# A fused gated-recurrence and ternary feed-forward block on one core: one weight on another DMA queue, powers ahead of constants, transposes in halves, another order around the second sequence

## The chip, the cores and the metric

The kernel runs on one core of one Trainium2 chip, in one launch. The metric is the device time in microseconds (us) of an execution. The kernel before takes 77.18 us, the median of 3 runs (77.08 to 77.36).

## What is computed

The input x holds 2 sequences of 512 tokens with 256 features, in float32. It is normalised once over its features, and two branches read the result:

```python
xn = (x - mean) / sqrt(var + eps)
# branch 1: gated linear recurrence
y    = gelu(xn @ w_y + b_y)
xb   = xn @ w_x + b_x
conv = conv_b + sum_k conv_w[k] * xb shifted by (3 - k) tokens     # 4 taps
gate_x, gate_a = sigmoid(conv @ w_ig + b_ig), sigmoid(conv @ w_ag + b_ag)
a    = exp(-8 * gate_a * softplus(a_param));  mult = sqrt(1 - a**2)
h_t  = a_t * h_{t-1} + gate_x * conv * mult                        # scan over tokens
attn = (h * y) @ w_out + b_out
# branch 2: feed-forward with ternary weights, hidden size 682
g    = silu(xn @ q(w1).T) * (xn @ q(w3).T)
out  = x + attn + g @ q(w2).T
```

## The kernel before

All is on chip after one load. Five engines each have a hand-written list of instructions, and semaphores tie them: an engine executes its list in order, and a wait in it holds all that stands behind. The source gives one function per engine: `sync` (SP, which issues nearly all DMAs), `gpsimd` (POOL), `scalar` (ACT), `vector` (DVE) and `tensor` (PE).

Exact products are made from a high part and a low part: a value v is rounded to a high part (on ACT), and the low part is v minus it. So there are `xt_hi`, `xt_lo` (the transposed, normalised x), `w_hi`, `w_lo` (five 256x256 weights, numbered WX, WY, WIG, WAG, WOUT) and `conv_hi`, `conv_lo`. A dense product is w_hi with the high part, w_lo with the high part and w_hi with the low part, accumulated in PSUM.

The start, per sequence s (4 tiles of 128 tokens):

1. DVE takes `statistics` (L437) and `variance` (L442, L445) of tiles; POOL raises v_eps to the power -0.5 (`rstd_of`, L231); DVE writes xn (`normalise`, L450). For s = 0 this goes in two halves of two tiles, each with its own power; for s = 1 in one piece, after one DMA for the whole sequence (L188).
2. PE transposes xn against the identity (`transposes`, L642, two per tile); ACT makes xt_hi of each half of the sequence (`xt_hi_of`, L288), DVE xt_lo of it (`xt_lo_of`, L456).
3. PE makes xb: for s = 0 in `first_x_terms` (L749, 256 columns at a time, 24 matmuls), for s = 1 in `dense_terms` (L653). ACT evicts xb with the newest tap and a bias (`newest_tap`, L317), DVE adds the other three taps (`older_taps(s, c)`, L489 and L493, one chunk c of 128 features at a time), ACT rounds it (`conv_hi_of`, L342) and POOL subtracts (`lo_of_conv`, L251).

POOL also makes small constants of the conv (`conv_constants`, L238 to L247: eight operations of 128x2, of which `newest_tap` needs `conv_c` and `older_taps` needs `head`) and `half_b` (L259), and the low parts of the weights (`square_lo`, L226). ACT rounds the weights (`square_hi`, L283) as they land. PE does 12 warm-up matmuls on ones and two more between waits (L722) before its first transpose.

The lists around the change, in the order of execution:

- SP: 4 tiles of x[0], WX, all of x[1], WY, WIG, WAG, w1, w3, w2, WOUT.
- POOL: `conv_constants`, `half_b`, two powers, (wait for xn of s = 0) `square_lo(WX)`, the power of s = 1, `square_lo(WY)`, `square_lo(WIG)`, `square_lo(WAG)`, four `lo_of_conv`.
- ACT: `square_hi(WX)`, `xt_hi_of(0)`, `square_hi(WY)`, `newest_tap(0)`, `square_hi(WIG)`, `xt_hi_of(1)`, the sum of absolute values of w1 (L300), `square_hi(WAG)`, `conv_hi_of(0, 0)`, the same sum of w3, `newest_tap(1)`, `conv_hi_of(0, 1)`, and on with gelu, tanh, exp.
- DVE: statistics and normalise of s = 0, statistics of s = 1, `xt_lo_of(0)`, `normalise(1)`, two tiny operations, `older_taps(0, 0)`, `xt_lo_of(1)`, `older_taps(0, 1)`, `older_taps(1, 0)`, `older_taps(1, 1)`, the thresholds and ternary weights (L460 to L505).
- PE: warm-up, transposes of s = 0, w_hi and w_lo with xt_hi, then w_hi with xt_lo for xb of s = 0; for y of s = 0 w_hi and w_lo with xt_hi, the transposes of s = 1, w_hi with xt_lo; then xb and y of s = 1, and the gates. The second gate of s = 0 reuses the PSUM of xb of s = 1 and so waits for the last `older_taps`.

After the gates come the hidden products of the feed-forward branch (L670), g (DVE, L515), its high and low parts (ACT L338, POOL L256), a tail of 42 hidden units (`tail_lo`, L573), and the products with w2 (`down`, L703) and w_out (L714).

Of the kernel before, what the change touches and what calls it, by code (L numbers as in the profile page):

```python
# [19 lines left out]
P = 128  # L20
# [5 lines left out]
KC = D // P  # L26
# [7 lines left out]
WARM = 12  # L34
# [9 lines left out]
def build(nc: bass.Bass, x, dense, w13t, w2t, params, b_out, out):  # L44
# [7 lines left out]
    with ctx:  # L52
# [85 lines left out]
        x_loaded = [sem(f"x_loaded{i}") for i in range(TILES + 1)]  # L138
# [42 lines left out]
        def _(sp):  # L181
# [5 lines left out]
            square(WX)  # L187
            sp.dma_start(x_sb[:, 1], x_dram[1]).then_inc(x_loaded[TILES], 16)  # L188
# [24 lines left out]
        def _(pool):  # L213
# [19 lines left out]
            def conv_constants():  # L233
# [24 lines left out]
            conv_constants()  # L258
            nc.gpsimd.tensor_scalar(half_b[:, :], par[:, B_IG:B_IG + 2 * KC], 0.5, None, ALU.mult).then_inc(half_b_set, 1)  # L259
            rstd_of(0, slice(0, TILES // 2), 1)  # L260
            rstd_of(0, slice(TILES // 2, TILES), 2)
            pool.wait_ge(xn_set, TILES)
            square_lo(WX)
            rstd_of(1, slice(0, TILES), 3)
            square_lo(WY)
            square_lo(WIG)
# [162 lines left out]
        def _(dve):  # L429
# [155 lines left out]
            dve.wait_ge(x_loaded[TILES], 16)  # L585
            statistics(1, range(TILES))
            variance(1, range(TILES))
            xt_lo_of(0)
            normalise(1, range(TILES), 3)
# [46 lines left out]
        def _(pe):  # L636
            def transposes(s):

                for t in range(TILES):
# [7 lines left out]
            def dense_terms(dst, m, terms, first, last, chunk_ready=None):  # L647
                for c in range(KC):
# [71 lines left out]
            def warm(count):  # L720
                for _ in range(count):
                    nc.tensor.matmul(slot[WARM_SLOT][:, 0, 0:P], ones[:, :], ones[:, :], start=True, stop=True)  # L722
# [20 lines left out]
            def first_x_terms(weights, part, ready):  # L743
                for h in range(2):
                    pe.wait_ge(ready, h + 1)
                    for c in range(KC):
                        for o in range(KC):
                            for w in weights:
                                mm = nc.tensor.matmul(slot[X_SLOT[0]][:, o, halves[h]], w[:, WX, c, o * P:(o + 1) * P],  # L749
                                                      part[:, 0, c, halves[h]],  # L750
                                                      start=(part is xt_hi and h == 0 and c == 0 and w is w_hi),
                                                      stop=(part is xt_lo and c == KC - 1), skip_group_check=True)
# [91 lines left out]
```

## Time and profile before

| | us |
|---|---|
| median of 3 runs | 77.18 (77.08 to 77.36) |
| the profiled execution, its own time | 77.82 |
| span of its trace, first to last instruction | 76.0 |
| busy: PE, DVE, ACT, POOL | 70.0, 60.8, 49.9, 33.4 |

The profile is of one execution. It has a page of summaries, and the trace behind it answers finer questions: the busy time of each engine in a stretch, the chain of instructions that ended last, and the instructions in order of time with their waits. Matmuls are pipelined: a matmul's stated duration holds its modelled end, so the pace is read from the distance between starts. The granted clock is 1.00 throughout.

### The profile page before, as it was taken

To read this page: it belongs to the slowest core of one execution; us is meant where nothing else is said; L and a number is where in the kernel's file an instruction comes from. 1 tells how busy PE (TensorE), PEld (TensorE's weight loads), DVE (VectorE), ACT (ScalarE), POOL (GpSimd) and SP (SyncE) were. 2 spreads that over 40 slices of the span, in tenths; PEclk is the share of its full clock that TensorE was granted. 3 is DMA by queue.
4 is the path that set the end of the run, shared out by engine and by line. 5 is a ranking of instruction groups with operands and counts; after the bars stand their busy time and mean duration, and the time that the engine had idled before them with its cause. 6 is when DMAs were issued, how large, how long until landed. Compare 5 with 4: busy or idle time off the path is not lost.

```text
span 76.0 us, 1062 instructions
## 1 busy us (share of the span) xinstructions
PE 70.0 (92%) x364; PEld 60.1 (79%) x364; DVE 60.8 (80%) x99; ACT 49.9 (66%) x76; POOL 33.4 (44%) x43
## 2 busy tenths in 40 slices
PE   4999879999999799999999999499999999999960
PEld 4999768877887678888888889388888888899950
DVE  4887599999999999999989999169999999400340
ACT  3663714899999999999989768996357429100000
POOL 6385646336661750052007968940007818910000
DMA  0989999910000000000000000000000000340062
GB/s 13 259 212 338 349 405 367 361 67 9 0 0 0 4 0 0 0 0 0 5 1 0 0 9 0 0 0 0 0 0 0 0 0 0 111 165 9 0 207 69
DMA packets 5095, 5.63 MB, mean 74 GB/s; under 512 B 525, under 2 KB 4578, under 8 KB 5090
## 3 DMA queue, kind: packets, MB, share of 16 engines
q1 hardware_dynamic: 4946, 5.55, 21.8%
q8 instruction: 3, 0.05, 0.2%
q10 hardware_dynamic: 144, 0.01, 0.1%
q14 instruction: 2, 0.02, 0.1%
HBM read 4.51 MB, written 1.05 MB: 73 GB/s over the span
## 4 chain that ended last, share of the span: by engine, by line
PE 37%; ACT 33%; DVE 9%; DMA 7%; issue 5%; POOL 3%; SPq 3%; DVEq 0%; ACTq 0%
PE slot L670 12%; PE slot L703 11%; PE slot L714 9%; DMA x_sb<-x 7%; ACT ta L363 4%; POOL g_lo L256 3%; ACT tx L349 3%; ACT conv_hi L342 3%; ACT xn_y L324 3%; PE slot L653 2%; ACT ta L355 2%; SPq L186 2%; ACT g_hi L300 2%; DVE w_raw L515 2%; DVE stats L437 2%
## 5 line engine op out<-in xcount | busy, mean ns | idle before, releaser
L256 POOL TENSOR_TENSOR g_lo<-w_raw,g_hi 128x512 fp32r<-128x512 f32 x10 | 15.9, 1609 | 16.1 <-ACT g_hi L338 16.1
L670 PE MATMUL slot<-xt_lo,w_q 128*128 128x512 f32 x40 | 15.7, 394 | 0.0
L670 PE MATMUL slot<-xt_hi,w_q 128*128 128x512 f32 x40 | 15.7, 393 | 0.0
L703 PE MATMUL slot<-w_q,g_hi 128*128 128x256 f32 x40 | 10.2, 292 | 1.1 <-POOL g_lo L256 1.1
L703 PE MATMUL slot<-w_q,g_lo 128*128 128x256 f32 x40 | 9.8, 282 | 0.0
L332 ACT ACTIVATE w_raw<-slot,scale 128x512 f32<-128x512 f32 x10 | 6.8, 686 | 4.3 <-PE slot L670 4.3
L493 DVE SCALAR_TENSOR_TENSOR conv<-slot,par,conv 128x511 f32<-128x511 f32 (+2 forms) x12 | 9.0, 748 | 0.4
L703 PEld LDWEIGHTS slot<-w_q,g_hi 128*128 128x128 f32 x40 | 7.6, 191 | 1.6 <-POOL g_lo L256 1.6
L670 PEld LDWEIGHTS slot<-xt_lo,w_q 128*128 128x128 f32 x40 | 7.5, 188 | 1.7
L670 PEld LDWEIGHTS slot<-xt_hi,w_q 128*128 128x128 f32 x40 | 7.5, 188 | 1.7
L338 ACT ACTIVATE g_hi<-w_raw 128x512 fp32r<-128x512 f32 x10 | 6.3, 630 | 3.4 <-DVE w_raw L515 3.2
L552 DVE TENSOR_TENSOR x_sb<-slot,x_sb 128x512 f32<-128x512 f32 (+1 forms) x5 | 2.8, 581 | 6.8 <-PE slot L703 6.8
L703 PEld LDWEIGHTS slot<-w_q,g_lo 128*128 128x128 f32 x40 | 7.6, 191 | 0.1
L515 DVE SCALAR_TENSOR_TENSOR w_raw<-w_raw,s,slot 128x512 f32<-128x512 f32 x10 | 7.2, 740 | 0.4 <-ACT w_raw L332 0.4
L226 POOL TENSOR_TENSOR w_lo<-w_raw,w_hi 128x512 fp32r<-128x512 f32 x4 | 5.1, 1287 | 4.6 <-ACT w_hi L283 4.6
L722 PE MATMUL slot<-ones 128*128 128x128 f32 x28 | 6.2, 420 | 1.0 <-POOL ones L214 1.0
L714 PE MATMUL slot<-w_raw,tx 128*128 128x256 f32 x32 | 7.1, 379 | 0.0
L653 PE MATMUL slot<-conv_hi,w_hi 128*128 128x512 f32 x16 | 6.4, 401 | 0.5 <-DVE conv L493 0.5
L251 POOL TENSOR_TENSOR conv_lo<-conv,conv_hi 128x512 fp32r<-128x512 f32 x4 | 5.4, 1343 | 3.4 <-ACT conv_hi L342 3.4
L722 PEld LDWEIGHTS slot<-ones 128*128 128x128 f32 x28 | 6.0, 330 | 1.0 <-POOL ones L214 1.0
L714 PEld LDWEIGHTS slot<-w_raw,tx 128*128 128x128 f32 x32 | 6.1, 190 | 0.9
L653 PE MATMUL slot<-conv_hi,w_lo 128*128 128x512 f32 x16 | 6.3, 394 | 0.0
(105 smaller groups left out, 143.1 us busy)
## 6 DMA issues: line engine op xcount, KB each, us to landing
w_raw<-w13t SPq DMA_DIRECT2D x2, 682.0 KB, 8.1
w_raw<-dense SPq DMA_DIRECT2D x5, 256.0 KB, 5.7
out<-x_sb SPq DMA_DIRECT2D x3, 256.0 KB, 2.2
w_raw<-w2t SPq DMA_DIRECT2D x1, 640.0 KB
x_sb<-x SPq DMA_DIRECT2D x4, 128.0 KB, 2.2
x_sb<-x SPq DMA_DIRECT2D x1, 512.0 KB, 5.4
out<-x_sb SPq DMA_DIRECT2D x2, 128.0 KB, 1.7
w_raw<-w2t SPq DMA_DIRECT2D x2, 42.0 KB
```

The source lines that it names most:

```text
L226: nc.gpsimd.tensor_tensor(w_lo[:, m], w_raw[:, m], w_hi[:, m].bitcast(f32), ALU.subtract).then_inc(w_lo_set, 1)
L251: nc.gpsimd.tensor_tensor(conv_lo[:, s, c], conv[:, s, c], conv_hi[:, s, c].bitcast(f32), ALU.subtract).then_inc(conv_lo_set, 1)
L256: nc.gpsimd.tensor_tensor(g_lo[:, j, s], g[:, n % RING], g_hi[:, j, s].bitcast(f32), ALU.subtract).then_inc(g_lo_set, 1)
L332: nc.scalar.activation(silu[:, n % RING], slot[H_SLOT[s][j]][:, 0], ACT.Silu, scale=scale[:, 0:1]).then_inc(silu_set, 1)
L338: nc.scalar.activation(g_hi[:, j, s], g[:, n % RING], ACT.Copy).then_inc(g_hi_set, 1)
L493: nc.vector.scalar_tensor_tensor(out=conv[:, s, c, i:], in0=slot[X_SLOT[s]][:, c, 0:SEQ - i], scalar=par[:, CONV_W + KC * k + c:CONV_W + K ...
L515: nc.vector.scalar_tensor_tensor(out=g[:, n % RING], in0=silu[:, n % RING], scalar=s32[:, 0:1], in1=slot[H_SLOT[s][j]][:, 1], op0=ALU.mult ...
L653: mm = nc.tensor.matmul(dst[:, o], w[:, m, c, o * P:(o + 1) * P], v[:, c], start=(first and i == 0 and c == 0), stop=(last and i == len(te ...
L670: mm = nc.tensor.matmul(slot[H_SLOT[s][j]][:, o], w13_q[:, c, col:col + P], v[:, s, c], start=(c == 0 and v is xt_hi), stop=(c == KC - 1 a ...
L703: mm = nc.tensor.matmul(out_tile(s, i, t), v[:, s, rows], w2_q[:, j], start=(first and j == 0 and t == tiles.start and k == 0), stop=(not ...
L714: mm = nc.tensor.matmul(out_tile(s, i, t), tx[:, s, c, t * P:(t + 1) * P], w_raw[:, WOUT, c], start=(first and c == 0 and t == tiles.start ...
L722: nc.tensor.matmul(slot[WARM_SLOT][:, 0, 0:P], ones[:, :], ones[:, :], start=True, stop=True)
```

## The change

It does these things:

- the load of WX goes from SP's queue to ACT's, right behind the small parameters; x[1] is loaded as two halves with a semaphore each;
- POOL's `conv_constants` is split: `tap_biases` (six small operations) stays ahead of the powers of s = 0, `head_sums` (three) goes between `square_lo(WX)` and `square_lo(WY)`; `half_b` goes behind the powers of s = 0; the power of s = 1 comes in two halves, behind `square_lo(WY)` where one stood ahead of it;
- PE warms up with 11 matmuls ahead and one of 64 columns between the halves of the first transposes, without waits on DVE and POOL; transposes of both sequences go in halves;
- for xb of s = 0, the product with the first half of xt_lo stands ahead of those with w_lo; for y of s = 0, both products with w_hi come first and those with w_lo are put around the second half of the transposes of s = 1;
- DVE does `xt_lo_of(0)` ahead of the statistics of s = 1, statistics and normalise of s = 1 in halves, and `xt_lo_of(1)` ahead of `older_taps(0, 0)`.

```diff
-WARM = 12
+WARM = 11
@@ SP
-            square(WX)
-            sp.dma_start(x_sb[:, 1], x_dram[1]).then_inc(x_loaded[TILES], 16)
+            for i in range(2):
+                t = slice(i * TILES // 2, (i + 1) * TILES // 2)
+                sp.dma_start(x_sb[:, 1, t], x_dram[1][:, t]).then_inc(x_loaded[TILES + i], 16)
@@ POOL
-            conv_constants()
-            nc.gpsimd.tensor_scalar(half_b[:, :], par[:, B_IG:B_IG + 2 * KC], 0.5, None, ALU.mult).then_inc(half_b_set, 1)
+            tap_biases()
             rstd_of(0, slice(0, TILES // 2), 1)
             rstd_of(0, slice(TILES // 2, TILES), 2)
+            nc.gpsimd.tensor_scalar(half_b[:, :], par[:, B_IG:B_IG + 2 * KC], 0.5, None, ALU.mult).then_inc(half_b_set, 1)
             pool.wait_ge(xn_set, TILES)
             square_lo(WX)
-            rstd_of(1, slice(0, TILES), 3)
+            head_sums()
             square_lo(WY)
+            rstd_of(1, slice(0, TILES // 2), 3)
+            rstd_of(1, slice(TILES // 2, TILES), 4)
             square_lo(WIG)
@@ ACT
             act.dma_start(par[:, :], params).then_inc(par_loaded, 16)
+            act.dma_start(w_raw[:, WX], dense[WX].rearrange("(c p) n -> p c n", p=P)).then_inc(w_loaded[WX], 16)
@@ DVE
-            dve.wait_ge(x_loaded[TILES], 16)
-            statistics(1, range(TILES))
-            variance(1, range(TILES))
             xt_lo_of(0)
-            normalise(1, range(TILES), 3)
+            for i in range(2):
+                dve.wait_ge(x_loaded[TILES + i], 16)
+                statistics(1, tile_halves[i])
+                variance(1, tile_halves[i])
+            for i in range(2):
+                normalise(1, tile_halves[i], i + 3)
...
+            xt_lo_of(1)
             older_taps(0, 0)
-            xt_lo_of(1)
             older_taps(0, 1)
@@ PE
             pe.wait_ge(ones_set, 1)
-            warm(WARM)
-            pe.wait_ge(mv_set, TILES)
-            warm(1)
-            pe.wait_ge(rstd_set, 1)
-            warm(1)
+            warm(WARM, P)
             pe.wait_ge(ident_set, 1)
-            transposes(0)
+            transposes(0, first_half)
+            warm(1, P // 2)
+            transposes(0, second_half)
...
             pe.wait_ge(w_hi_set, WX + 1)
-            first_x_terms((w_hi,), xt_hi, xt_hi_set)
+            for h in range(2):
+                first_x_terms((w_hi,), xt_hi, xt_hi_set, h)
+            first_x_terms((w_hi,), xt_lo, xt_lo_set, 0)
             pe.wait_ge(w_lo_set, WX + 1)
-            first_x_terms((w_lo,), xt_hi, xt_hi_set)
-            first_x_terms((w_hi,), xt_lo, xt_lo_set).then_inc(xb_psum, 1)
+            for h in range(2):
+                first_x_terms((w_lo,), xt_hi, xt_hi_set, h)
+            first_x_terms((w_hi,), xt_lo, xt_lo_set, 1).then_inc(xb_psum, 1)
             pe.wait_ge(w_hi_set, WY + 1)
-            dense_terms(slot[Y_SLOT[0]], WY, [(w_hi, xt_hi[:, 0])], True, False)
+            dense_terms(slot[Y_SLOT[0]], WY, [(w_hi, xt_hi[:, 0]), (w_hi, xt_lo[:, 0])], True, False)
+            transposes(1, first_half)
             pe.wait_ge(w_lo_set, WY + 1)
-            dense_terms(slot[Y_SLOT[0]], WY, [(w_lo, xt_hi[:, 0])], False, False)
-            transposes(1)
-            dense_terms(slot[Y_SLOT[0]], WY, [(w_hi, xt_lo[:, 0])], False, True).then_inc(y_psum, 1)
+            dense_terms(slot[Y_SLOT[0]], WY, [(w_lo, xt_hi[:, 0])], False, True, chunks=[0])
+            transposes(1, second_half)
+            dense_terms(slot[Y_SLOT[0]], WY, [(w_lo, xt_hi[:, 0])], False, True, chunks=[1]).then_inc(y_psum, 1)
```

## Rows read from the trace of the kernel before

**Rows 1.** The page, chain that ended last: shares of the span by engine.
```profile
PE 37%; ACT 33%; DVE 9%; DMA 7%; issue 5%; POOL 3%; SPq 3%; DVEq 0%; ACTq 0%
```

**Rows 2.** Busy us (instructions) of PE, PEld, DVE, ACT, POOL; clock, DMA, GB/s.
```profile
18.00:38.00 20.00, 19.47 (x87) 15.82 (x87) 19.67 (x27) 19.92 (x32) 7.79 (x6) 1.00 0.00 1
```

**Rows 3.** Instructions in order of time, late: start, us, instruction [idle before, releaser].
```profile
38.96 1.41 DVE L515 SCALAR_TENSOR_TENSOR w_raw<-w_raw,s,slot 128x512 f32<-128x512 f32 x2 [0.36 <-ACT w_raw L332]
...
46.67 1.22 DVE L573 TENSOR_TENSOR gt<-w_raw,gt_hi 42x1024 fp32r<-42x1024 f32 x1
46.72 2.29 POOL L256 TENSOR_TENSOR g_lo<-w_raw,g_hi 128x512 fp32r<-128x512 f32 x1 [0.36 <-ACT g_hi L338]
49.07 0.38 PE L703 MATMUL slot<-w_q,g_hi 128*128 128x256 f32 x1 [1.11 <-POOL g_lo L256]
```

**Rows 4.** The same view, start of the first sequence, DVE and POOL.
```profile
3.28 0.75 DVE L437 BATCH_NORM_STATS2 stats<-x_sb 128x6 f32<-128x256 f32 x2
4.22 0.47 POOL L244 TENSOR_TENSOR head<-head,b_tap 128x2 f32<-128x2 f32 x2
4.36 0.75 DVE L437 BATCH_NORM_STATS2 stats<-x_sb 128x6 f32<-128x256 f32 x2
5.12 1.54 POOL L231 TENSOR_TENSOR rstd<-v_eps,power 128x2 f32<-128x2 f32 x2
5.36 0.17 DVE L445 TENSOR_SCALAR v_eps<-mv 128x2 f32<-128x2 f32 x1
5.88 1.54 DVE L450 TENSOR_SCALAR xn_y<-x_sb,mv,rstd 128x256 f32<-128x256 f32 x4 [0.36 <-POOL rstd L231]
```

**Rows 5.** DMA issues in 2.5 to 3.03, us to landing; below, a busy stretch (columns as rows 2).
```profile
w_raw<-dense SPq DMA_DIRECT2D x1, 256.0 KB, 4.2
x_sb<-x SPq DMA_DIRECT2D x1, 128.0 KB, 2.3
...
2.00:3.00 1.00, 1.00 (x6) 1.00 (x6) 0.73 (x2) 0.44 (x1) 0.00 (x0) 1.00 1.04 261
```

**Rows 6.** Instructions in order of time, PE and ACT up to the second transposes.
```profile
7.65 1.09 ACT L288 ACTIVATE xt_hi<-slot 128x512 fp32r<-128x512 f32 x2 [0.19 <-PE slot L642]
8.39 1.19 PE L749 MATMUL slot<-xt_hi,w_hi 128*128 128x256 f32 x8 [0.34 <-ACT xt_hi L288]
9.15 0.63 ACT L283 ACTIVATE w_hi<-w_raw 128x512 fp32r<-128x512 f32 x1 [0.42 <-DMA w_raw<-dense]
9.42 1.12 PE L749 MATMUL slot<-xt_hi,w_lo 128*128 128x256 f32 x8
12.20 1.09 PE L653 MATMUL slot<-xt_hi,w_hi 128*128 128x512 f32 x4
12.47 1.45 ACT L317 ACTIVATE conv<-slot,conv_c,par 128x512 f32<-128x512 f32 x2 [2.68 <-PE slot L749]
14.04 1.04 PE L642 MATMUL slot<-ident,xn_y 128*128 128x128 f32 x8
14.84 1.17 PE L653 MATMUL slot<-xt_lo,w_hi 128*128 128x512 f32 x4
```

**Rows 7.** The same view, POOL and DVE around the second normalise (its first tile).
```profile
11.43 1.28 POOL L226 TENSOR_TENSOR w_lo<-w_raw,w_hi 128x512 fp32r<-128x512 f32 x1
11.50 1.36 DVE L450 TENSOR_SCALAR xn_y<-x_sb,mv,rstd 128x256 f32<-128x256 f32 x1
```

**Rows 8.** The same view, DVE and ACT from the second transposes to the first conv.
```profile
14.02 0.16 DVE L489 TENSOR_TENSOR conv<-conv,head 128x3 f32<-128x3 f32 x1
14.68 1.09 ACT L288 ACTIVATE xt_hi<-slot 128x512 fp32r<-128x512 f32 x2 [0.25 <-PE slot L642]
16.45 1.28 DVE L456 TENSOR_TENSOR xt_lo<-slot,xt_hi 128x512 fp32r<-128x512 f32 x2
17.50 0.63 ACT L342 ACTIVATE conv_hi<-conv 128x512 fp32r<-128x512 f32 x1
17.64 0.15 DVE L489 TENSOR_TENSOR conv<-conv,head 128x3 f32<-128x3 f32 x1
```

More of the change, by code:

```diff
@@ L135, in xt_bank @@
             return slot[T_SLOT[s]][:, h].rearrange("p (c n) -> p c n", c=KC)
-        x_loaded = [sem(f"x_loaded{i}") for i in range(TILES + 1)]
+        x_loaded = [sem(f"x_loaded{i}") for i in range(TILES + 2)]
         w_loaded = [sem(f"w_loaded{m}") for m in range(5)]
@@ L231, in rstd_of, with tap_biases @@
                 nc.gpsimd.tensor_tensor(rstd[:, s, tiles], v_eps[:, s, tiles], power[:, tiles], ALU.pow).then_inc(rstd_set, 1)
-            def conv_constants():
+            def tap_biases():
                 b_x = par[:, B_X:B_X + KC]
@@ L241, in conv_constants, with head_sums @@
                 nc.gpsimd.tensor_tensor(conv_c[:, 0], b_tap[:, TAPS - 1], par[:, CONV_B:CONV_B + KC], ALU.add).then_inc(conv_c_set, 1)
+            def head_sums():
                 for k in range(1, TAPS - 1):
@@ L636, in _, with transposes @@
         def _(pe):
-            def transposes(s):
-                for t in range(TILES):
+            def transposes(s, tiles):
+                for t in tiles:
                     pe.wait_ge(xn_set, TILES * s + t + 1)
@@ L645, in transposes, with dense_terms @@
                         mm.then_inc(xt_psum, 1)
-            def dense_terms(dst, m, terms, first, last, chunk_ready=None):
-                for c in range(KC):
+            def dense_terms(dst, m, terms, first, last, chunk_ready=None, chunks=range(KC)):
+                for c in chunks:
                     if chunk_ready:
@@ L718, in project, with warm @@
                             mm.then_inc(o_psum, 1)
-            def warm(count):
+            def warm(count, cols):
                 for _ in range(count):
-                    nc.tensor.matmul(slot[WARM_SLOT][:, 0, 0:P], ones[:, :], ones[:, :], start=True, stop=True)
+                    nc.tensor.matmul(slot[WARM_SLOT][:, 0, 0:cols], ones[:, :], ones[:, 0:cols], start=True, stop=True)
+            first_half, second_half = range(0, TILES // 2), range(TILES // 2, TILES)
             pe.wait_ge(ones_set, 1)
-            warm(WARM)
-            pe.wait_ge(mv_set, TILES)
-            warm(1)
-            pe.wait_ge(rstd_set, 1)
-            warm(1)
+            warm(WARM, P)
             pe.wait_ge(ident_set, 1)
-            transposes(0)
+            transposes(0, first_half)
+            warm(1, P // 2)
+            transposes(0, second_half)
             def sums_of_w13():
@@ L741, in sum_of_w2, with first_x_terms @@
                 nc.tensor.matmul(sum2, ones[:, :], abs_sum[:, 2:4], start=True, stop=True).then_inc(sum2_psum, 1)
[L743 to L752, printed above, removed]
+            def first_x_terms(weights, part, ready, h):
+                pe.wait_ge(ready, h + 1)
+                for c in range(KC):
+                    for o in range(KC):
+                        for w in weights:
+                            mm = nc.tensor.matmul(slot[X_SLOT[0]][:, o, halves[h]], w[:, WX, c, o * P:(o + 1) * P],
+                                                  part[:, 0, c, halves[h]],
+                                                  start=(part is xt_hi and h == 0 and c == 0 and w is w_hi),
+                                                  stop=(part is xt_lo and h == 1 and c == KC - 1), skip_group_check=True)
```

## The prediction

> **What bounds the kernel now.** I began with the chain of work that ended last. PE has 37% of it and ACT 33% [rows 1], and in order of time ACT has nearly all of it from the second transposes to the forties, PE all of it from 49 us. So no one engine bounds the kernel. The busy time by stretch says more: from 18 to 38 us ACT, DVE and PE are each busy for 97 to 100% [rows 2]. Three full engines that feed each other pass a delay on at full size, and pass a gain on only if all three start earlier. The late waits fit this [rows 3]: DVE at 38.96 had waited for ACT (0.36 us), PE at 49.07 for POOL (1.11 us), whose low part of g hangs on DVE and ACT. Behind 49 us PE runs nearly unbroken to the end. All that the change edits lies ahead of 18 us. The question is therefore one: when do ACT and DVE enter the full stretch? In the instructions in order of time the entry is `conv_hi_of(0, 0)` on ACT at 17.50 and `older_taps(0, 1)` on DVE at 17.64 [rows 8]. I compute both.
>
> **The change part by part.** All times are of the profiled trace.
>
> *Powers ahead of the constants.* v_eps of the second half ends at 5.36 + 0.17 = 5.53, that of the first 1.08 earlier (as its statistics start, 3.28 against 4.36), at 4.45; POOL begins the two powers only at 5.12, 0.77 us each [rows 4]. With `head_sums` (from 4.22) and `half_b` gone POOL is free at 4.3, so the first power runs 4.5 to 5.27, the second waits for DVE and runs 5.56 to 6.33. Then two tiles remain to normalise: 0.33 us apart and 0.41 long (four took 1.54 with one wait between). xn of sequence 0 would be complete at 6.38 + 0.74 = 7.1, where it was at 5.88 + 1.54 = 7.42. It can't be earlier: DVE is what v_eps waits for.
>
> *WX on ACT's queue.* Its issue costs ACT some 0.43 us at 1.13, ahead of a table load that is done before the parameters land; nothing waits for that. WX landed at 2.57 + 4.2 = 6.8 and now lands some 1.5 us earlier, ahead of its use at 8 us. The price is on x: the last tile of x[0] was issued at 2.10, landed 2.3 us later, at 4.4 [rows 5], and its statistics start at 4.70 (the second of two in 0.75 us from 4.36, [rows 4]); slack 0.3. The DMA engines are full at 261 GB/s in this stretch [rows 5], so 256 KB more among the x tiles take up to 1.0 us of it; with none of it on the last tile the cost is zero. I take 0.5, the middle, less the slack of 0.3: xn complete at 7.3, between 7.1 and 7.8. The Trainium skill ("DMA: Bandwidth & Descriptors", Issuing engines are not separate DMA queues) says that DMAs started from any engine run on the same 16 DMA engines and interleave, so that a second queue saves issue time alone. By that the whole 1.0 us would fall on x and the sum below would be 0.45 us more.
>
> *Shorter warm-up, halves of transposes.* PE's first transpose ran at 7.0, behind the warm-up, though xn's first tile was there at 6.3. That frees the first half; the second half sets the pace, and it hangs on xn. From xn complete to ACT's second xt_hi: transposes and hand-over 0.67 (in sequence 1 ACT follows the first of four transposes by 14.68 - 14.04 = 0.64, [rows 6, 8]), ACT 0.60, hand-over to PE 0.14 (ACT ended the first half at 8.25, PE began at 8.39, [rows 6]). So the second half of w_hi with xt_hi starts at 7.3 + 1.41 = 8.7.
>
> *First half of xt_lo ahead of w_lo, low parts ahead of statistics.* From there PE has 20 matmuls of 256 columns, 0.94 us for 8 at their pace (9.42 to 10.36): 2.35 us. Before, PE stopped here for DVE, whose xt_lo stood behind the statistics. `square_lo(WX)` starts as before behind xn, ends at about 8.7 and is needed at 9.65: hidden, with 0.9 us of cover. xb is complete at 11.05, where it was at 12.20: a gain of 1.1 us.
>
> *Up to xt_hi of sequence 1.* PE: 8 matmuls of y 1.84 (12.20 to 14.04), four transposes 0.40 (eight from 14.04 to 14.84), two matmuls with w_lo 0.46, the last transposes to ACT 0.64, ACT 0.60 [rows 6, 8]: 3.94 us. xt_hi of sequence 1 is complete at 15.0, where it was at 14.68 + 1.09 = 15.77. The gain has shrunk from 1.1 to 0.8, since two of y's matmuls with w_lo now stand between the halves of the transposes.
>
> *Is xn of sequence 1 ready for it?* DVE's statistics now start at 9.3 behind xt_lo; each half takes 1.1, so v_eps is done at 11.5 (it was 10.38). The powers stand behind `square_lo(WY)`, which ends at 11.1 (WY landed at 9.15, ACT 0.63, POOL 1.28, [rows 6, 7]). Two powers: 12.65. Normalise to 13.45, where it was 13.83. PE wants the halves at 12.9 and 13.8: ready, with 0.2 to 0.4 us of cover. `head_sums` (0.7 us of POOL) fits ahead of WY.
>
> *`xt_lo_of(1)` ahead of `older_taps(0, 0)`.* This is the term that decides. Before, DVE began `older_taps(0, 0)` at 14.02, during PE's transposes and ACT's xt_hi, and took xt_lo at 16.45: no time was lost in waiting. Now DVE, free at 13.7, must wait for both halves of xt_hi, to 15.0. The second xt_lo takes 0.67 with hand-over; `older_taps(0, 0)` starts at 15.7 and ends 2.51 later, at 18.2. ACT's `conv_hi_of(0, 0)`, which ACT's own work (17.50 lay 1.73 us behind xt_hi) would allow at 16.75, starts at 18.25: 0.75 us later than 17.50. `older_taps(0, 1)` starts at 18.2: 0.55 later than 17.64 [rows 8]. The next one waits for ACT's `newest_tap(1)`, which carries ACT's 0.75, so DVE takes on the same. PE's X and Y of sequence 1 are a little earlier, but the gates wait for conv.
>
> **Sum.** ACT and DVE enter the full stretch 0.75 us late; with a handful of hand-overs I take 0.8. No slack behind it is larger than the 0.36 of DVE at 38.96, and that is a wait for ACT, which is the late one. Span 76.0 + 0.8 = 76.8; the profiled execution lay 1.82 above its span, at 77.82, and the median of the runs 0.64 below it. So the same change on the median: 77.18 + 0.8 = 78.0 us. By the bounds: with x not delayed at all (7.1) the term is 0.6, with WX wholly in the way (7.8) 1.25. That gives 77.8 to 78.4 for this case. Break-even would need xn of sequence 0 at 6.5, ahead of what DVE's statistics allow.
>
> **Rivals.**
>
> *1. A port race on the second normalise.* In the trace, the first tile of that normalise took 1.36 us instead of 0.41, and ended when POOL's `square_lo(WY)`, begun 0.07 us before it, did [rows 7]. Now `square_lo(WY)` (9.8 to 11.1) lies over DVE's first v_eps of sequence 1 (10.4), and `square_lo(WIG)` may start at 13.25 (xb 11.05, hand-over 0.25, `newest_tap` 1.34 from its start to the next, 0.63; [rows 6]), 0.2 us behind the issue of the last tile at 13.05. If v_eps is held as a large tile is, it loses 0.7, its powers and tiles go to 13.9, and the last tile then does fall behind `square_lo(WIG)`, to some 14.9. xt_hi is complete at 16.1 instead of 15.0: 1.1 more, 79.0 us (78.6 to 79.3). Against it: v_eps has two elements per partition, and no row shows such a one held. The Trainium skill ("SBUF — State Buffer", Who interferes with whom) calls it an exclusive lock, held for the whole instruction, of GpSimd against a VectorE instruction in a 2-port mode, tensor_scalar among them. The 1.36 us agree; by it the small one would wait as well.
>
> *2. WX in the way.* x is late by the whole 1.0 us (and the load does not do what its move is for): 78.4 us.
>
> *3. The late port race turns.* At 46.7 DVE's `tail_lo` starts 0.05 us before POOL's low part of g, which then takes 2.29 us instead of 1.28, and PE waits 1.11 us [rows 3]. A shift of 0.05 us between DVE and ACT reverses this. If POOL then also keeps its next product ahead of `tail_lo`, PE gains the 1.1 us: with the 0.6 of the lower bound, 77.18 + 0.6 - 1.1 = 76.7 us, faster. It decides on whether ACT's `g_hi_of(3)` ends before DVE's g of n = 4 does. Against it: both follow the same instruction of DVE, so their distance should stay; and if DVE gets its turn in between, the wait only moves.
>
> *4. The delay is swallowed.* Busy shares hide short waits; if ACT had hidden slack between 18 and 38 us, of 0.3 us or more, the entry would cost little: 77.2 us (76.8 to 77.6). For it: engine busy times overlap by some hundredths at each hand-over. Against it: three engines would need it at the same time.
>
> **How the numbers follow.** Forecast (78.0) 0.40; rival 1 (79.0) 0.18; rival 2 (78.4) 0.10; rival 3 (76.7) 0.12; rival 4 (77.2) 0.20. Rivals 1 and 2 and the forecast lie above; a comparison of this kernel can tell about 0.5% from no change, 0.39 us, so slower means above 77.57 and faster below 76.8. Slower: 0.18 + 0.10 + 0.37 of the forecast = 0.65; the rest of the forecast, 0.03, and 0.17 of rival 4 are no change, 0.20; faster: rival 3 and 0.03 of rival 4, 0.15. The range that leaves out rival 3 and the end of rival 1 is 76.8 to 79.2.
>
> **What would show it.** In the profile after: xn of sequence 0 complete near 7.3; xb of sequence 0 at 11.05, 1.1 us earlier; xt_hi of sequence 1 near 15.0; DVE with a wait for ACT's xt_hi ahead of xt_lo, where it had none; ACT with a wait of over 1 us for DVE ahead of `conv_hi_of(0, 0)`, near 18.25; then everything to the end later by one amount. A normalise or v_eps of a microsecond shows rival 1; statistics of the last tile behind 5.0 rival 2; PE's wait before its fourth product with w2 gone, rival 3. The forecast is wrong if `conv_hi_of(0, 0)` is late and the end is not, or if xt_hi of sequence 1 is done by 14.3.

## The result, and the profile after

The changed kernel takes 79.54 us, the median of 4 runs (79.42 to 81.03), where the kernel before takes 77.25 (77.08 to 77.36). The ratio is 1.0293 (95% interval 1.0261 to 1.0326): slower by 2.3 us. I had forecast 78.0 with a range of 76.8 to 79.2. The direction was right, the size was not.

The execution of 81.03 us is one in which TensorE's clock fell (last section); it is left out of the ratio. The lines below are of the changed kernel run again, in an execution of 79.58 us with a span of 77.4. First the page, chain that ended last, and then the busy stretch with the columns of [rows 2]:

```profile
PE 32%; ACT 29%; DVE 17%; POOL 7%; issue 7%; DMA 3%; POOLq 0%; DVEq 0%; ACTq 0%
```

```profile
18.00:38.00 20.00, 18.48 (x80) 14.18 (x79) 19.34 (x29) 19.08 (x31) 7.66 (x6) 1.00 0.00 1
```

DVE's share of the chain has nearly doubled (9% in [rows 1]). In the same stretch PE is busy 0.99 us less than in [rows 2] and ACT 0.84 us less: ACT enters late. The start of the first sequence, in order of time, against [rows 4 and 6]:

```profile
4.03 0.43 DVE L444 BATCH_NORM_STATS2 stats<-x_sb 128x6 f32<-128x256 f32 x1 [0.33 <-DMA x_sb<-x]
...
5.04 0.81 DVE L444 BATCH_NORM_STATS2 stats<-x_sb 128x6 f32<-128x256 f32 x2 [0.16 <-DMA x_sb<-x]
...
6.74 0.67 PE L651 MATMUL slot<-ident,xn_y 128*128 128x128 f32 x4 [1.11 <-DVE xn_y L457]
...
7.17 0.73 DVE L457 TENSOR_SCALAR xn_y<-x_sb,mv,rstd 128x256 f32<-128x256 f32 x2 [0.26 <-POOL rstd L232]
```

The statistics of the second and third tile now wait for their x loads (none did in [rows 4]), and xn (the normalised x) of sequence 0 is complete at 7.90, where it was at 7.42. Then from the second statistics to the first conv, against [rows 6 to 8]:

```profile
9.68 0.74 DVE L444 BATCH_NORM_STATS2 stats<-x_sb 128x6 f32<-128x256 f32 x2
9.93 1.29 POOL L227 TENSOR_TENSOR w_lo<-w_raw,w_hi 128x512 fp32r<-128x512 f32 x1
10.67 0.57 DVE L452 TENSOR_SCALAR v_eps<-mv 128x2 f32<-128x2 f32 x1
11.59 0.40 PE L662 MATMUL slot<-xt_hi,w_hi 128*128 128x512 f32 x1
13.23 0.74 DVE L457 TENSOR_SCALAR xn_y<-x_sb,mv,rstd 128x256 f32<-128x256 f32 x2 [0.27 <-POOL rstd L232]
14.07 1.15 DVE L603 TENSOR_SCALAR a_rate<-sp_e 128x2 f32<-128x2 f32 x1
14.97 0.60 ACT L295 ACTIVATE xt_hi<-slot 128x512 fp32r<-128x512 f32 x1 [0.31 <-PE slot L651]
15.13 1.27 DVE L463 TENSOR_TENSOR xt_lo<-slot,xt_hi 128x512 fp32r<-128x512 f32 x2
16.33 0.14 DVE L496 TENSOR_TENSOR conv<-conv,head 128x3 f32<-128x3 f32 x1
18.86 0.63 ACT L349 ACTIVATE conv_hi<-conv 128x512 fp32r<-128x512 f32 x1 [1.44 <-DVE conv L500]
```

xb of sequence 0 is complete at 11.59 (PE's next product), xt_hi of sequence 1 at 14.97 + 0.60 = 15.57, `older_taps(0, 0)` starts at 16.33 and `conv_hi_of(0, 0)` at 18.86, 1.36 later than in [rows 8], with ACT idle for DVE 1.44 us ahead of it. Two operations of DVE on two elements per partition, the v_eps at 10.67 and `a_rate` at 14.07, take 0.57 and 1.15 us where v_eps takes 0.17 in [rows 4]; more on them below. The late race answers [rows 3]:

```profile
48.00 1.22 DVE L580 TENSOR_TENSOR gt<-w_raw,gt_hi 42x1024 fp32r<-42x1024 f32 x1
48.05 2.29 POOL L260 TENSOR_TENSOR g_lo<-w_raw,g_hi 128x512 fp32r<-128x512 f32 x1 [0.36 <-ACT g_hi L345]
...
50.40 0.39 PE L712 MATMUL slot<-w_q,g_hi 128*128 128x256 f32 x1 [1.08 <-POOL g_lo L260]
```

The distance of 0.05 us, POOL's 2.29 and PE's wait stand as before, all 1.33 later. Of a lateness of 1.36 at the entry, 1.33 is still there at 50 us and 1.4 in the span.

### The profile page after: what moved, and what is told of

Same layout as the page of the kernel before. It is cut to its first block, busy times and chain, and to the rows that moved or that the text cites. A ratio compares the mean times of both kernels' runs of the same rounds, so it can differ in the third digit from the quotient of the medians.

```text
span 78.8 us, 1058 instructions
## 1 busy us (share of the span) xinstructions
PE 70.3 (89%) x360; PEld 59.6 (76%) x360; DVE 60.9 (77%) x100; ACT 50.0 (63%) x76; POOL 33.9 (43%) x44
## 4 chain that ended last, share of the span: by engine, by line
PE 42%; ACT 28%; DVE 10%; issue 6%; DMA 5%; POOL 3%; SPq 2%; DVEq 0%; ACTq 0%
PE slot L679 12%; PE slot L712 10%; PE slot L723 9%; DMA x_sb<-x 5%; PE slot L756 5%; ACT ta L370 4%; PE slot L651 3%; POOL g_lo L260 3%; PE slot L662 3%; ACT tx L356 3%; DVE conv L500 3%; ACT xn_y L331 3%; ACT ta L362 2%; ACT conv_hi L349 2%; ACT g_hi L307 2%
## 5 line engine op out<-in xcount | busy, mean ns | idle before, releaser
L731 PE MATMUL slot<-ones 128*128 128x128 f32 (+1 forms) x24 | 4.9, 384 | 1.0 <-POOL ones L215 1.0
L731 PEld LDWEIGHTS slot<-ones 128*128 128x128 f32 x24 | 4.6, 295 | 1.0 <-POOL ones L215 1.0
```

Source lines behind the costliest of these rows:

```text
L731: nc.tensor.matmul(slot[WARM_SLOT][:, 0, 0:cols], ones[:, :], ones[:, 0:cols], start=True, stop=True)
```

## The experiments

My theory after the result: WX in front of x is dearer than I took it (1.6 us), the wait of `xt_lo_of(1)` costs what was forecast or more, and both undone give 77.1 us, the time of the kernel before. The rival: the rest of the change costs too, the second statistics behind the low parts above all (77.8 us or more). In this section "outside" is an execution's time less its span (a span is given to 0.1 us). The kernel before was run beside each group; over all it had medians of 77.04 to 77.6.

### Undoing parts of the change

The changed kernel again, without an edit:

> The changed kernel once more, for a trace in which TensorE's granted clock stays at 1.00. Theory A (x late, then DVE waits): the last tile of x[0] lands near 6.1 us as in the first trace of it, xn of sequence 0 is complete near 8.6, xb of sequence 0 at 12.3 (8.6 + 3.76), xt_hi of sequence 1 at 16.3, ACT's conv_hi(0, 0) starts at 19.5 and the time is 79.3 to 79.6. Theory B (PE's clock after the shorter warm-up is the cause): the trace shows the clock at 0.5 in some part again, and without it the time is near 78.

79.64 us (79.47 to 79.80), ratio 1.0275 (1.0227 to 1.0322), span 77.4. With a mean clock of 0.996 the time is that of the other executions, so the clock (theory B) isn't the cause. Theory A had the time right and its steps too late: xn is complete at 7.90, not 8.6, and conv starts at 18.86, not 19.5. WX back on SP's queue, behind the x tiles:

```diff
-            act.dma_start(w_raw[:, WX], ...)
...
             for t in range(TILES): sp.dma_start(x_sb[:, 0, t], ...)
+            square(WX)
```

> The changed kernel with the load of WX back on SP's queue, behind the four tiles of x[0]. Theory A: the tiles land as before the change (the last at 4.4), xn of sequence 0 is complete at 7.15, xt_hi of sequence 1 at 14.85, conv_hi(0, 0) starts at 18.1: 77.9 us, against 79.5 with the move. Rival (the queue is not the cause, the second statistics or the order is): 79 or more.

78.90 us, ratio 1.0186 (1.0139 to 1.0233), span 76.7, where I had expected 77.9. The instructions in order of time:

```profile
6.43 0.74 DVE L457 TENSOR_SCALAR xn_y<-x_sb,mv,rstd 128x256 f32<-128x256 f32 x2 [0.26 <-POOL rstd L233]
...
18.12 0.63 ACT L349 ACTIVATE conv_hi<-conv 128x512 fp32r<-128x512 f32 x1 [1.45 <-DVE conv L500]
...
21.95 1.28 ACT L331 ACT_TABLE_LOAD   x1
```

xn is complete at 7.17 and `conv_hi_of(0, 0)` starts at 18.12, each 0.73 or 0.74 earlier; the time falls by 0.74. That is the price of WX in front of x, under half of what I had expected; the rest of the loss sits elsewhere. The same lines of before show how the rest passes through: its gelu table load starts at

```profile
21.34 1.28 ACT L324 ACT_TABLE_LOAD   x1
```

and this one at 21.95, 0.61 later, as 18.12 is 0.62 later than 17.50; the next loads (36.88 and 37.49) keep the 0.61. Then `xt_lo_of(1)` back behind `older_taps(0, 0)`, alone and with WX on SP:

```diff
-            xt_lo_of(1)
             older_taps(0, 0)
+            xt_lo_of(1)
```

> The changed kernel with xt_lo of sequence 1 behind older_taps(0, 0) again. Theory A: DVE takes the first taps in PE's and ACT's time; older_taps(0, 1) starts near 18.6 where it was 17.64 before the change, conv_hi(0, 0) near 18.0: 78.2 us. Rival (the late x alone is the cause, DVE's order is worth nothing): 79.5 us as changed.

> The changed kernel with both taken back: WX on SP's queue, xt_lo of sequence 1 behind older_taps(0, 0). Theory A: older_taps(0, 1) starts near 17.5, conv_hi(0, 0) earlier than 17.50 by up to 0.9: 77.1 us, level with the kernel before. Rival (the rest of the change, the second statistics behind the low parts above all, costs too): 77.8 or more.

80.17 us (1.0349, 1.0286 to 1.0412) and 79.54 (1.0262, 1.0218 to 1.0305): each 0.5 to 0.6 slower than its partner that keeps the edit. I had expected 78.2 and 77.1, so my theory fell here: taking the deciding term away should have given time back. The trace of the second of them, in order of time:

```profile
13.15 1.29 POOL L228 TENSOR_TENSOR w_lo<-w_raw,w_hi 128x512 fp32r<-128x512 f32 x1 [0.71 <-ACT w_hi L290]
13.32 1.15 DVE L603 TENSOR_SCALAR a_rate<-sp_e 128x2 f32<-128x2 f32 x1
14.39 0.15 DVE L496 TENSOR_TENSOR conv<-conv,head 128x3 f32<-128x3 f32 x1
16.92 0.63 ACT L349 ACTIVATE conv_hi<-conv 128x512 fp32r<-128x512 f32 x1 [0.25 <-DVE conv L500]
17.98 1.29 POOL L256 TENSOR_TENSOR conv_lo<-conv,conv_hi 128x512 fp32r<-128x512 f32 x1
18.00 1.29 DVE L496 TENSOR_TENSOR conv<-conv,head 128x3 f32<-128x3 f32 x1
18.14 1.19 PE L662 MATMUL slot<-xt_lo,w_hi 128*128 128x512 f32 x4 [1.15 <-DVE xt_lo L463]
```

`conv_hi_of(0, 0)` did come 1.2 us earlier than with the edit (16.92 against 18.12). But two operations of two and three elements per partition took 1.15 and 1.29 us, where the same ones take 0.17 and 0.15 alone, and both end with a POOL operation that had begun 0.17 and 0.02 us before them (1.15 and 1.30 us in the other kernel of the two). The hold of `a_rate` stands in the traces with the edit too (1.15 us), but there DVE has to wait for xt_hi anyway. In the kernel before, the head add, the first operation of `older_taps(0, 1)`, starts at 17.64 [rows 8], and POOL's operation next to it is a low part of a weight:

```profile
17.69 1.30 POOL L226 TENSOR_TENSOR w_lo<-w_raw,w_hi 128x512 fp32r<-128x512 f32 x1 [1.89 <-ACT w_hi L283]
```

DVE wins by 0.05 us (by 0.01 us in a second profile of that kernel), and `a_rate` runs there before POOL's low part begins. So the old order doesn't just lack a wait, it is on the good side of both races, and the new timing of POOL puts it on the bad side.

### Is it the race? The tiny operations moved out of its way

The version with both edits undone, and the softplus sum with `a_rate` ahead of the second statistics:

```diff
             xt_lo_of(0)
+            sp_e[:, 1] ...; a_rate ...
             for i in range(2): statistics(1, ...) ...
```

> The changed kernel with WX back on SP, xt_lo of sequence 1 behind older_taps(0, 0), and also DVE's two tiny operations (softplus sum and a_rate) moved ahead of the second statistics. It differs from a3_both by that alone. In a3_both a_rate (128x2) took 1.15 us beside POOL's square_lo(WIG). If that hold is what the old order cost there, older_taps(0, 0) starts near 13.4 instead of 14.4 and the time falls by up to 1.0, to 78.5; its first operation of chunk 1 may still be held by POOL. If the hold is not a cause, 79.5 as a3_both.

Ten runs in groups: 77.31, 77.35, 77.35; 78.3; 79.07, and five from 79.44 to 79.65. I had expected 78.5. The profiled one (77.35, span 75.1) shows both head adds beside POOL and neither held:

```profile
13.13 0.15 DVE L496 TENSOR_TENSOR conv<-conv,head 128x3 f32<-128x3 f32 x1
13.14 1.30 POOL L228 TENSOR_TENSOR w_lo<-w_raw,w_hi 128x512 fp32r<-128x512 f32 x1 [0.70 <-ACT w_hi L290]
...
16.56 0.62 ACT L349 ACTIVATE conv_hi<-conv 128x512 fp32r<-128x512 f32 x1
16.74 1.33 POOL L228 TENSOR_TENSOR w_lo<-w_raw,w_hi 128x512 fp32r<-128x512 f32 x1 [2.29 <-ACT w_hi L290]
16.75 0.15 DVE L496 TENSOR_TENSOR conv<-conv,head 128x3 f32<-128x3 f32 x1
```

The starts are within 0.01 us, the first in DVE's favour, the second in POOL's by the record, so which came first can't be read there. One kernel has two times 2.1 us apart, and the longer one is that of the version above, whose trace (span 77.2 against 75.1) shows both holds. That the races are lost in the executions near 79.5 us, no trace of them shows; it is tested by the next kernel, which decides the races by a wait:

```diff
+            pool.wait_ge(tap_step, 1)
             square_lo(WIG)
+            pool.wait_ge(tap_step, 1 + (TAPS - 1))
             square_lo(WAG)
```

> a4_rate_early with two waits on POOL: square_lo(WIG) behind the first operation of older_taps(0, 0), square_lo(WAG) behind that of older_taps(0, 1). a4_rate_early took 77.3 us in three of ten executions and 79.4 to 79.65 in five; in the profiled one, at 77.35, the first operations of DVE's taps began 0.01 us ahead of POOL's. Theory P (in the slow executions POOL came first and held DVE's two-input operations for 1.3 us each): with the waits every execution takes 77.2 to 77.5. Rival (something else makes the two groups): both groups stay.

77.2 us (76.88 to 77.35, 12 runs), ratio 0.9978 (0.9949 to 1.0008), as expected. The group near 79.5 us is gone. POOL now follows the head add (13.60, then 13.84):

```profile
10.19 0.78 DVE L454 TENSOR_SCALAR v_eps<-mv 128x2 f32<-128x2 f32 x1
...
13.60 0.16 DVE L498 TENSOR_TENSOR conv<-conv,head 128x3 f32<-128x3 f32 x1
...
13.84 1.29 POOL L228 TENSOR_TENSOR w_lo<-w_raw,w_hi 128x512 fp32r<-128x512 f32 x1 [0.92 <-DVE conv L498]
...
16.56 0.62 ACT L351 ACTIVATE conv_hi<-conv 128x512 fp32r<-128x512 f32 x1
```

It is the fastest version of the changed kernel, level with the kernel before (76.75 to 78.43 beside it) and narrower, not measurably faster. Its span, 75.1 to 75.6, is no shorter than that of the three 77.3 us executions without the waits (75.1 to 75.2); it has less outside the span (below). The spans also give the price of the order: 76.7 with `xt_lo_of(1)` early, 75.1 with it late and `a_rate` out of POOL's way, 1.6 us, and the two holds cost 2.1, which is why taking back the edit alone lost time. Two versions took such a pair of waits (the first of them ahead of `square_lo(WY)`) into the old kernel, with `transposes(1)` ahead of y's low parts on PE; the first also moved `a_rate` ahead of the second statistics:

```diff
+            pool.wait_ge(tap_step, 1)
             square_lo(WY)
             square_lo(WIG)
+            pool.wait_ge(tap_step, 1 + (TAPS - 1))
             square_lo(WAG)
...
+            transposes(1)
+            dense_terms(..., [(w_hi, xt_lo[:, 0])], False, False)
             pe.wait_ge(w_lo_set, WY + 1)
```

> The kernel before with POOL kept away from DVE's short operations: a_rate ahead of the second statistics, square_lo(WY) behind the first operation of older_taps(0, 0), square_lo(WAG) behind that of older_taps(0, 1), and on PE the transposes of sequence 1 and the product with xt_lo ahead of that with w_lo. If the held normalise (1.36 instead of 0.41 us) is what starts the full stretch late, xn of sequence 1 is complete 0.9 us earlier, ACT's conv_hi(0, 0) 0.8 earlier, and the time is 76.4 to 76.8 us. Rival (ACT or PE are the bound there, the hold is hidden): 77.3.

> The kernel before with square_lo(WY) behind the first operation of older_taps(0, 0) and square_lo(WAG) behind that of older_taps(0, 1), and PE's transposes of sequence 1 and the product with xt_lo ahead of that with w_lo; a_rate stays in its place. Theory P: the normalise of sequence 1 isn't held (four tiles in 1.4 us instead of 2.35), older_taps(0, 0) starts at 12.5, ACT's conv_hi(0, 0) at 16.3 where it was 16.8 to 17.5, and the time is 76.4 to 77.0 us. Rival: ACT is the bound there, the time is that of before, 77.3 to 77.6.

78.06 us (1.0054, 1.0023 to 1.0085) and 77.94 (1.0066, 1.0031 to 1.0101), where I had expected 76.4 to 77.0. With `a_rate` moved, it met `square_lo(WX)` instead:

```profile
7.47 1.27 POOL L226 TENSOR_TENSOR w_lo<-w_raw,w_hi 128x512 fp32r<-128x512 f32 x1 [0.85 <-DVE xn_y L452]
7.49 1.27 DVE L591 TENSOR_SCALAR a_rate<-sp_e 128x2 f32<-128x2 f32 x1
...
8.68 1.40 DVE L439 BATCH_NORM_STATS2 stats<-x_sb 128x6 f32<-128x256 f32 x4
...
11.68 1.38 DVE L452 TENSOR_SCALAR xn_y<-x_sb,mv,rstd 128x256 f32<-128x256 f32 x4
```

The last line is what the held-back POOL buys: the second normalise takes 1.38 us where it took 2.34. `conv_hi_of(0, 0)` came at 17.31 and 17.16, without an idle time of ACT ahead of it, so ACT is the bound there. The second of them had x[1] at 8.52; the old kernel with x[1] at 8.52 has conv at 17.52 (next part), so of the 0.96 us on the normalise 0.36 arrived. In the medians not even that is seen (spans of 75.9 and 75.75, those of the kernel before beside them 75.75 and 75.7), which stays open, and both kernels carry 0.4 us more outside.

### Single parts put into the kernel before

The kernel before itself, as a control; WX on ACT's queue alone; an unused semaphore; x[1] as two loads, both awaited in the old place:

> The kernel before, unedited, for a second profile of it. The changed kernel's executions lie 2.1 to 2.2 us above their spans, the profiled execution of before 1.8 above its span of 76.0. Theory C (the part outside the span grew with the change): before lies again 1.8 above its span, whatever the execution, so the median 77.2 to 77.4 has a span of 75.5. Rival: it lies 2.1 to 2.2 above it, and the span of a median execution is near 75.2. ACT's conv_hi(0, 0) starts at 17.5 in both.

> The kernel before with one edit: the load of WX on ACT's queue. Theory A as corrected by the traces: the last tile of x[0] lands 0.9 to 1.7 us later (at 5.3 to 6.1), xn of sequence 0 is complete 0.5 to 1.2 us later; but PE waits for xt_lo behind the second statistics in this kernel, and DVE's statistics wait for x[1] until 8.49, so most of it is covered: 77.2 to 77.7 us. Rival (nothing covers it): 78.0 to 78.4.

> The kernel before with one more semaphore, which nothing uses. If the part outside the span grows with the semaphores that the program holds (theory C's first guess), the time rises by some 0.3 us; if not, it is that of before within 0.1 us.

> The kernel before with x[1] loaded as two DMAs, and DVE waiting for both before its statistics as before. If the split makes the part outside the span longer, this kernel lies 2.1 to 2.2 us above its span instead of 1.8, and takes about 77.6 to 77.8 us; if not, it is as before, 77.3 within 0.3, and 1.8 above its span.

77.67 us (1.0016, 0.9976 to 1.0056), 77.44 (1.0007, 0.9964 to 1.0049), 77.48 (0.9970, 0.9925 to 1.0015) and 77.15 (0.9967, 0.9931 to 1.0003), all near what was expected. None of these parts costs anything that can be told from noise here, WX included. WX's trace says why: xn is late (complete at 7.23 + 0.73 = 7.96), but the second statistics begin right at its end, at 7.88, without a wait for x[1], and `conv_hi_of(0, 0)` starts at 16.95. In the control the load of x[1] is what they wait for, in the third kernel less so:

```profile
8.52 1.08 DVE L437 BATCH_NORM_STATS2 stats<-x_sb 128x6 f32<-128x256 f32 x3 [1.09 <-DMA x_sb<-x]
...
17.52 0.63 ACT L342 ACTIVATE conv_hi<-conv 128x512 fp32r<-128x512 f32 x1
```

```profile
7.74 1.41 DVE L437 BATCH_NORM_STATS2 stats<-x_sb 128x6 f32<-128x256 f32 x4 [0.42 <-DMA x_sb<-x]
...
16.73 0.63 ACT L342 ACTIVATE conv_hi<-conv 128x512 fp32r<-128x512 f32 x1
```

The same instructions, x[1] 0.78 us earlier, conv 0.79 earlier, the span 75.2 instead of 76.0. With the split load it is 7.79, 16.81 and 75.3, in the profile that I predicted from 8.49, 17.50 and 76.0: one for one. Two later kernels with old lists fit as well, the one with idle waits (7.99, 16.98 and 75.5) and the one with the shorter warm-up (8.71, 17.72 and 76.2). The old kernel's runs spread from 76.7 to 78.8 us; that the landing of x[1] is behind all of this spread is argued from these profiles, not shown for the runs without one. The profile that I predicted from was a late one.

Then the two moves of low parts, each alone in the old kernel:

```diff
+            xt_lo_of(1)
             older_taps(0, 0)
-            xt_lo_of(1)
```

> The kernel before with one edit: xt_lo of sequence 1 ahead of older_taps(0, 0). By the prediction's reasoning xt_hi of sequence 1 is complete at 15.77 as before, DVE waits for it, older_taps(0, 0) starts at 16.4, ACT's conv_hi(0, 0) at 19.0 instead of 17.5: 78.7 us. Rival (DVE's later low parts cost PE more than this, as the changed kernel with the old order was slower by 0.6): 77.2 or less.

79.02 us (1.0153, 1.0079 to 1.0227; expected 78.7). DVE's line is now

```profile
14.19 1.29 DVE L456 TENSOR_TENSOR xt_lo<-slot,xt_hi 128x512 fp32r<-128x512 f32 x2 [1.18 <-ACT xt_hi L288]
...
17.94 0.63 ACT L342 ACTIVATE conv_hi<-conv 128x512 fp32r<-128x512 f32 x1 [1.44 <-DVE conv L493]
```

although its second statistics began at 7.39. One for one, the old order would have its conv at 16.4 there, and at 16.7 even with nothing gained below 7.74; so the edit alone costs 1.2 us or more. This is the deciding term, shown by itself.

```diff
+            xt_lo_of(0)
             dve.wait_ge(x_loaded[TILES], 16)
             statistics(1, range(TILES)); variance(1, range(TILES))
-            xt_lo_of(0)
```

> The kernel before with one edit: xt_lo of sequence 0 ahead of the statistics of sequence 1, in one piece. Theory D (a kernel whose second statistics stand behind xt_lo no longer gains from an early x[1], and its power comes late): statistics start at 9.4 whenever x[1] lands, v_eps is done at 11.3, the power at 12.35, normalise is held by POOL's square_lo(WY) to the end of that near 13.6 and is complete at 14.7; older_taps(0, 0) starts at 15.0, against 13.3 to 14.0 before: 78.7 us. Rival (low parts first frees PE earlier and pays for itself): 77.3 or less.

79.68 us (1.0277, 1.0233 to 1.0320), as much as the whole change and 1 us more than I had expected. The second statistics go from 8.5 to 9.45, and then

```profile
12.38 2.56 POOL L226 TENSOR_TENSOR w_lo<-w_raw,w_hi 128x512 fp32r<-128x512 f32 x2
12.45 3.29 DVE L450 TENSOR_SCALAR xn_y<-x_sb,mv,rstd 128x256 f32<-128x256 f32 x4 [1.12 <-POOL rstd L231]
...
13.71 1.19 PE L653 MATMUL slot<-xt_hi,w_lo 128*128 128x512 f32 x4 [1.30 <-POOL w_lo L226]
```

the normalise meets two low parts of POOL back to back. The change avoids this by its halved powers behind `square_lo(WY)`; this part of it is a repair of its own edit.

PE's new list, and the shorter warm-up (its edit is the one below), each in the old kernel:

```diff
-            warm(WARM); pe.wait_ge(mv_set, TILES); warm(1); pe.wait_ge(rstd_set, 1); warm(1)
+            warm(WARM - 1)
```

> The kernel before with PE's whole list of the changed kernel, and nothing else of the change. PE waits for the first half of xt_lo (10.2) ahead of the products with w_lo, so y starts at 12.1 instead of 11.4 and xt_hi of sequence 1 is complete about 1.0 later, with two matmuls between the halves of the transposes: 78.2 us. For the part outside the span: if PE's list makes it longer, it is 2.1 to 2.3 us here; if not, 1.8.

> The kernel before with the shorter warm-up alone: 11 matmuls and no waits for DVE and POOL between. PE then idles from 5.7 to the first tile of xn at 6.3, and the first transposes are done 0.6 us earlier; xt_lo stands behind the second statistics, so nothing of it reaches the end: 77.3 us, clock at 1.00. If PE's clock fell for the gap, matmuls of 256 columns would take twice their 0.117 us from start to start. The part outside the span: 1.8, or 2.1 to 2.3 if the warm-up is what makes it longer.

PE's whole list, without DVE's new order, gives 78.66 us (1.0156, 1.0090 to 1.0221; expected 78.2): in the profiled execution, whose x[1] landed very late (9.06), PE waits 2.10 us for `xt_lo_of(0)`, which still stands behind the statistics. The warm-up alone gives 77.48 (0.9982, 0.9936 to 1.0028): its first transpose starts at 6.32, and nothing comes of it. The 7.0 that I predicted from is no price of the old warm-up either: in the control it starts at 6.45, and at 6.33 in the kernel with the unused semaphore.

### The part outside the span

The changed kernel had 2.13 to 2.23 us outside, the kernel before 1.74 to 1.93, in every execution. The semaphore, the split load, WX's queue, the warm-up and PE's list all kept 1.74 to 1.93; so did the two moves of low parts. The other versions of the changed kernel had 2.14 to 2.32, except the one with two waits on POOL (1.75 to 1.90), while both old kernels with two waits on POOL (and PE's order changed) had 2.13 to 2.31. So I added two POOL waits that never hold anything, to each kernel:

```diff
+            pool.wait_ge(xn_set, TILES)
             square_lo(WIG)
+            pool.wait_ge(xn_set, TILES)
             square_lo(WAG)
```

> Two waits of POOL on a count that was reached long ago (the normalised x of sequence 0), one ahead of each of its last two low parts, in the kernel before. Nothing waits longer for them, so the span should stay where that of the kernel before is, 75.2 to 76.2 us. If the time outside the span hangs on how many waits POOL's queue holds, it goes from 1.8 to 2.2 us here (as in the two kernels that held the low parts back) and the time to about 77.9; if it hangs on what POOL really waits for, or on the order of PE, it stays at 1.8 and the time at 77.5.

> The same two idle waits of POOL in the changed kernel. Span as the changed kernel's, 77.2 to 77.6. If the number of waits in POOL's queue sets the time outside the span, it may go back from 2.2 to 1.8 us, as it did between the two kernels that differed by POOL's two waits alone, and the time to 79.2; otherwise it stays at 2.2 and the time at 79.6.

| | time | span | outside |
|---|---|---|---|
| before with idle waits, 4 runs | 77.50 to 77.70 | 75.3 to 75.5 | 2.19 to 2.29 |
| before beside it, 5 runs | 76.69 to 77.24 | 74.9 to 75.4 | 1.74 to 1.87 |
| after with idle waits, 2 runs | 79.22, 80.28 | 77.4, 78.5 | 1.82, 1.78 |
| after, 8 runs | 79.42 to 81.03 | 77.2 to 78.8 | 2.13 to 2.23 |

The idle waits leave the span alone and switch the outside part by 0.4 us, up in one kernel and down in the other. In these pairs it hangs on the content of POOL's list, not on the schedule; which part of the change moved it was not tested. Why the same two waits go both ways stays open: no row of the profile lies in that part.

## Why the prediction was right or wrong

The miss of 79.54 - 78.0 = 1.54 us has three terms. The second is shown by an experiment; the first is read from profiles, and the third is measured without a known cause.

*"So the same change on the median: 77.18 + 0.8": wrong by about 0.6.* The sum was made against a profile of span 76.0, and I moved it to the median as if both kernels shared what made that execution slow. They don't. It was the late x[1] (8.49), on which the old kernel's conv hangs one for one; in the new kernel the second statistics stand behind `xt_lo_of(0)`, at 9.68 here and 8.93 with WX on SP, behind any landing seen but the very late 9.06. So the old kernel's median has a span of 77.25 - 1.8 = 75.4, the new one's gains nothing from an early x[1]: at a full clock its spans lie between 77.2 and 77.6, those of the old one between 74.9 and 76.9. The 0.64 between the profiled execution and the median was in the text, without the question of what it was made of. It was the first row to ask about: DVE's wait ahead of the second statistics.

*WX on ACT's queue: term mis-sized, 0.2 taken net of the slack, 0.73 measured.* "xn complete at 7.3, between 7.1 and 7.8": it was 7.90, and 7.17 without the move. The forecast spent the slack of 0.3 at the last tile only. In the rows more tiles than the last are late (x landed 3.1 us after issue in the median, against 2.2 before), and the delays in DVE's list add up: the statistics of the second tile start 0.4 us later, those of the third 0.68 (5.04 instead of 4.36), and the second v_eps starts at 6.11 instead of 5.36. The rule that the prediction cited from the Trainium skill ("DMA: Bandwidth & Descriptors", Issuing engines are not separate DMA queues) gave the whole 1.0 us on x, 0.7 net: it would have been nearer (7.8) than the middle that I took, and the trace agrees with it. This is rival 2, and it came true in addition to the base, not in its place.

*The part outside the span: 0.37, not in the sum at all.* 2.19 against 1.82. I had taken the 1.82 us of the one profiled execution as the same in both kernels without saying so.

Together 0.57 + 0.61 + 0.37 = 1.55 us, with 0.57 for 76.0 - 75.43, and 0.61 for 18.86 against the 18.25 forecast. That it meets 1.54 to 0.01 is partly luck: the forecast's rounding of 0.75 to 0.8 and its older median (77.18 for 77.25) nearly cancel with the small differences that are left.

*What held.* From xn complete on, the steps were right to some hundredths: xb complete 3.69 us after xn (3.76 worked out), xt_hi of sequence 1 another 3.98 (3.94), `older_taps(0, 0)` 0.76 behind that (0.7), conv 2.53 on (2.55). With WX on SP and xn at 7.17 the formulas give a conv at 7.17 + 3.76 + 3.94 + 0.7 + 2.55 = 18.12; it was 18.12. `xt_lo_of(1)` ahead of `older_taps(0, 0)` costs what it was said to: ACT idle 1.44 us for DVE, alone 1.2 us or more in the old kernel. And lateness at the entry passed on nearly whole, 0.61 of 0.62 with WX on SP, so rival 4 (delay swallowed, 0.20) is out. Rival 3 is out as its counter-argument said: both sides of the race moved together.

*Rival 1, the port race, came true in part.* I doubted that a v_eps of two elements can be held, since no row showed one. It took 0.57 and 0.78 us instead of 0.17, `a_rate` 1.15 and 1.27, a head add 1.29. The Trainium skill ("SBUF — State Buffer", Who interferes with whom) calls the shared pair an exclusive lock for the whole instruction, and says that the order of issue decides, not the shape; the trace agrees with 1.15 and 1.29 us for 128x2 and 128x3. In the changed kernel the holds were covered: behind v_eps its xn of sequence 1 was ready, behind `a_rate` DVE had to wait for xt_hi, and the big tiles were not held (0.74 for two). But the race is why the edit that my sum blamed could not be undone by itself: the old order in the new timing costs two holds, 2.1 us, and saves 1.6.

## What to carry to other kernels

Before a difference worked out on one profiled execution is moved to a median, find the row that makes this execution slower than the median (here a load's landing), and ask whether the changed kernel would still wait for it. A load on a second queue is not free for the loads that it overtakes: price it on every tile that its consumer takes as it lands. Where a DVE operation of any size and a POOL one start within some 0.1 us of each other, treat the order as undecided, price both outcomes, and settle it with a wait if the kernel's time depends on it.

## What the runs showed of the hardware that I had not expected

An operation of two elements per partition is held by POOL as long as a large one: 1.27 us for a `tensor_scalar` of 128x2, 1.29 for a `tensor_tensor` of 128x3 with both inputs in SBUF. A kernel with such pairs 0.01 us apart had two groups of times, 77.3 and 79.5 us, and two executions between them.

Two waits that never hold changed the time around the span by 0.4 us, from 1.8 to 2.2 in one kernel and from 2.2 to 1.8 in the other, in every execution.

TensorE's clock: in two of ten executions of the changed kernel (with the one with idle waits), it was granted half for a while. With PE idle for 2.06 us ahead of its first transpose the changed kernel's first profile shows

```profile
7.41 0.73 PE L651 MATMUL slot<-ident,xn_y 128*128 128x128 f32 x4 [2.06 <-DVE xn_y L457]
...
9.09 2.26 PE L756 MATMUL slot<-xt_hi,w_hi 128*128 128x256 f32 x8
```

and in the view of busy time by stretch

```profile
8.00:11.50 3.50, 3.50 (x18) 3.30 (x18) 2.68 (x8) 1.71 (x3) 2.67 (x6) 0.53 1.00 369
```

a granted clock of 0.53 from 8.0 to 11.5, close to 1.2 GHz of 2.4, and eight matmuls in 2.26 us where [rows 6] have 1.19; the time was 81.03 us. The other one had an idle time of 1.86 us, 0.57 and 80.28 us. In the execution with 1.11 us of idle time the mean clock was 0.996, in the old kernel with the shorter warm-up and 0.98 us it was 0.999. Both falls came with the shorter warm-up and WX in front of x together, in 2 of 14 executions that have both (the four with the late `xt_lo_of(1)` counted in); with one of the two alone, 10 executions each in the old kernel kept a mean clock of 0.996 or more. So the waits of the old warm-up may cover a cost that shows only in some executions; no run here isolates it.
